# A selective scan with nine turned states, re-laid orders, and a row-wise walk of the column directions

## What is computed

```python
x_trans = jnp.transpose(xc, (0, 1, 3, 2)).reshape(Bn, Din, L)
x_hwwh = jnp.stack([x_flat, x_trans], axis=1)
xs = jnp.concatenate([x_hwwh, jnp.flip(x_hwwh, axis=-1)], axis=1)     # K = 4 directions
x_dbl = jnp.einsum('bkdl,kcd->bkcl', xs, x_proj_weight)
dts, Bs, Cs = jnp.split(x_dbl, [R, R + N], axis=2)                    # N = 16 states
delta = softplus(einsum(dts, dt_projs_weight) + dt_projs_bias)        # Din = 384
def step(h, inp):
    dA = jnp.exp(d_l[..., None] * A)
    dBu = d_l[..., None] * B_l[:, :, None, :] * u_l[..., None]
    h = dA * h + dBu
    y = jnp.sum(h * C_l[:, :, None, :], axis=-1)
```

## Time and profile before

| | |
|---|---|
| median of 3 runs | 28435.44 us (28420.39 to 28436.43) |
| the profiled execution | 28430.92 us |
| its span on the core | 28429.4 us |
| busy in the span: PE, DVE, ACT, POOL | 89%, 84%, 73%, 78% |
| mean granted TensorE clock | 0.944 of full speed |

### The profile page before, as it was taken

The page is one execution under the profiler, slowest core; times in us unless marked ns, Lnnn a source line. Parts: engine busy times, 40 slices in busy tenths (PEclk is TensorE's granted clock), DMA queues, the critical chain, the costliest instruction groups (busy, mean ns, idle before and its releaser), DMA issues. The chain is left out here.

```text
span 28429.4 us, 291694 instructions
## 1 busy us (share of the span) xinstructions
PE 25357.2 (89%) x80480; PEld 11869.3 (42%) x80480; DVE 23856.0 (84%) x23376; ACT 20735.5 (73%) x38376; POOL 22128.3 (78%) x9798
## 2 busy tenths in 40 slices
PE   8899888998889988899888998889988899888998
PEld 3444334443344433444334443344433444334443
DVE  6799867998679986799867998679986799867998
ACT  4788647886478864788647886478864788647886
POOL 3799737997379973799737997379973799737997
PEclk8999989999899998999989999899998999989999
DMA  0111101111011110111101111011110111101111
GB/s 8 51 63 64 45 8 51 63 64 45 8 51 63 63 46 8 51 63 63 46 8 51 63 63 46 8 51 63 64 45 8 51 63 64 45 8 51 63 64 45
DMA packets 833671, 1309.75 MB, mean 46 GB/s; under 512 B 224897, under 2 KB 242177, under 8 KB 828929
## 3 DMA queue, kind: packets, MB, share of 16 engines
q1 hardware_dynamic: 832000, 1290.45, 14.6%
HBM read 1223.00 MB, written 67.11 MB: 45 GB/s over the span
## 5 line engine op out<-in xcount | busy, mean ns | idle before, releaser
L1592 PE MATMUL ps<-arena,ident 128*128 128x512 f32 x24576 | 11670.0, 601 | 50.9 <-DVE arena L1419 50.8
L1407 DVE TENSOR_TENSOR_SCAN arena<-ps,arena 128x512 f32<-128x512 f32 x6144 | 7492.6, 1261 | 329.5 <-issue 208.0
L1407 DVE TENSOR_TENSOR_SCAN arena<-arena,ps 128x512 f32<-128x512 f32 x6144 | 7413.5, 1257 | 121.7 <-ACT arena L1786 101.9
L1960 POOL TENSOR_TENSOR arena<-arena 128x1536 f32<-128x1536 f32 x2048 | 7067.8, 3457 | 146.2 <-DVE arena L1407 144.6
L1592 PEld LDWEIGHTS ps<-arena,ident 128*128 128x128 f32 x24576 | 4349.8, 192 | 4544.5 <-issue 4240.7
L1970 POOL TENSOR_TENSOR arena<-arena 128x1536 f32<-128x1536 f32 x1728 | 5971.4, 3463 | 52.8 <-ACT arena L1806 52.8
L1797 ACT ACTIVATE scaled<-arena,cols 128x384 f32<-128x384 f32 x8192 | 4711.4, 605 | 1032.5 <-PE ps L1560 1025.5
L1786 ACT ACTIVATE ps<-arena 128x512 f32<-128x512 f32 x6144 | 4123.6, 684 | 602.2 <-DVE arena L1407 592.6
L1786 ACT ACTIVATE arena<-arena 128x512 f32<-128x512 f32 x6144 | 4251.2, 716 | 100.1 <-PE ps L1592 99.0
L1560 PE MATMUL ps<-ident,scaled 128*128 128x128 f32 x24576 | 3612.6, 277 | 590.3 <-DVE arena L1407 420.1
L1560 PEld LDWEIGHTS ps<-ident,scaled 128*128 128x128 f32 x24576 | 2854.6, 141 | 3050.1 <-DVE arena L1407 1583.7
(11 more groups left out here) (187 smaller groups left out, 32595.1 us busy)
## 6 DMA issues: line engine op xcount, KB each, us to landing
arena<-rows SPq DMA_DIRECT2D x3776, 256.0 KB, 3.2
spare<-rows SPq DMA_DIRECT2D x576, 256.0 KB, 3.4
arena<-x SPq DMA_DIRECT2D x16, 1536.0 KB, 13.0
x<-arena SPq DMA_DIRECT2D x16, 1536.0 KB, 10.7
arena<-x SPq DMA_DIRECT2D x64, 384.0 KB, 8.7
out<-arena SPq DMA_DIRECT2D x64, 384.0 KB, 3.0
rows<-xd SPq DMA_DIRECT2D x256, 64.0 KB, 2.7
arena<-L_conv_fc_w SPq DMA_DIRECT2D x16, 576.0 KB, 5.2
```

The lines of the kernel that those rows point to most:

```text
L1407: nc.vector.tensor_tensor_scan(flip(states(b, n, t)), flip(decays), flip(adds), carry[:, k, N2 * n + t:N2 * n + t + 1], ALU.mult, ALU.add) ...
L1592: nc.tensor.matmul(m.ps[:, t, :], m.ident[:, :], states(b, n, t), start=False, stop=(n == SUMS[t][-1])).then_inc(at[Y_MM[t]], 1)
L1960: nc.gpsimd.tensor_tensor(three(dbu[:, no % DB, :]), du[:, b % 2, :, :], each, ALU.mult).then_inc(at["db_ready"], 1)
```

## The change

Three things change, all in the scan.

1. TURNED grows from eight states to nine, (1, 3, 5, 6, 8, 9, 11, 13, 14). States 6 and 8 are new in it, 7 leaves. PLAIN is then (0, 2, 4, 7, 10, 12, 15). POOL_C keeps its nine states.
2. The per-block lists of all five engines and the orders SUMS are laid anew.
3. In the column directions the operands are walked by image rows. On the image side a pattern now reads eight neighbouring floats and jumps to the next row; its counterpart (PSUM for `rows_of`, `take_old` and `give_y`, SBUF for delta and du) is then stepped by 64 floats. Before, the image side was stepped by 64 floats and the counterpart was contiguous. The values are the same.

```diff
-TURNED = (1, 3, 5, 7, 9, 11, 13, 14)
+TURNED = (1, 3, 5, 6, 8, 9, 11, 13, 14)
-SUMS = ((1, 0, 2, 3, 4, 5, 6, 7, 8, 9, 10, 12, 11, 13, 14, 15),
...
+SUMS = ((0, 1, 2, 4, 3, 6, 5, 7, 8, 9, 10, 11, 12, 13, 14, 15),
...
         wide = T // H
-        return v.rearrange("p t (h w) -> p t w h", w=W)[:, t, i * wide:(i + 1) * wide, :]
+        return v.rearrange("p t (h w) -> p t h w", w=W)[:, t, :, i * wide:(i + 1) * wide]
 
     def shaped(b, v):
-        return v if b // NT % 2 == 0 else v.rearrange("p (w h) -> p w h", h=H)
+
+        return v if b // NT % 2 == 0 else v.rearrange("p (w h) -> p h w", h=H)
...
                 scan(b, 5, 2)
-                correct(ahead, 0)
-                times_c(b, 4)
                 scan(b, 6, 0)
                 scan(b, 6, 1)
                 scan(b, 6, 2)
+                correct(ahead, 0)
+                times_c(b, 4)
...
                 times_c(b, 0)
                 times_c(b, 1)
-                times_b(b, 6)
+                low_of(ahead)
+                times_b(b, 7)
                 times_c(b, 3)
-                times_b(b, 8)
+                times_b(b, 10)
                 softplus(ahead, 0, 0)
```

More of the change, by code:

```diff
@@ L1473, in _ @@
                 scan(b, 6, 2)
+                correct(ahead, 0)
+                times_c(b, 4)
                 scan(b, 7, 0)
                 scan(b, 7, 1)
[L1476 removed]
                 scan(b, 7, 2)
+                times_c(b, 6)
                 scan(b, 8, 0)
                 scan(b, 8, 1)
[L1480 removed]
                 scan(b, 8, 2)
+                correct(ahead, 1)
                 scan(b, 9, 0)
@@ L1596, in _ @@
                 past, ahead = b - 1, b + 1
+                add_up(past, 12, 2)
+                add_up(past, 12, 1)
+                rows_of(ahead, 0)
                 add_up(past, 11, 0)
-                rows_of(ahead, 0)
+                rows_of(ahead, 1)
                 turn_back(b, 1, 0)
-                rows_of(ahead, 1)
-                spread_c(past, 15)
+                rows_of(ahead, 2)
                 turn_back(b, 1, 1)
                 turn_back(b, 1, 2)
-                rows_of(ahead, 2)
+                add_up(past, 13, 2)
@@ L1613, in _ @@
                 turn_back(b, 3, 1)
                 turn_back(b, 3, 2)
+                take_old(b, 0)
+                spread_c(b, 2)
                 add_up(past, 14, 2)
                 add_up(past, 15, 1)
+                add_up(b, 0, 0)
                 delta_of(ahead, 0)
-                take_old(b, 0)
-                spread_c(b, 2)
-                add_up(past, 15, 2)
+                turn_back(b, 5, 0)
                 take_old(b, 1)
-                add_up(b, 1, 0)
-                turn_back(b, 5, 0)
@@ L1624, in _ @@
-                spread_c(b, 4)
                 turn_back(b, 5, 1)
                 turn_back(b, 5, 2)
-                add_up(b, 1, 1)
                 add_up(b, 0, 1)
                 take_old(b, 2)
+                add_up(b, 0, 2)
+                turn_back(b, 6, 0)
+                turn_back(b, 6, 1)
+                turn_back(b, 6, 2)
+                add_up(b, 2, 2)
+                spread_c(b, 4)
+                add_up(b, 1, 0)
+                add_up(b, 1, 1)
+                add_up(b, 1, 2)
@@ L1642, in _ @@
[L1642 to L1655, removed]
+                turn_back(b, 8, 0)
@@ new lines, in _ @@
+                add_up(b, 4, 0)
+                turn_back(b, 8, 1)
+                turn_back(b, 8, 2)
+                add_up(b, 3, 0)
+                spread_c(b, 8)
+                add_up(b, 4, 1)
+                add_up(b, 3, 1)
+                turn_back(b, 9, 0)
+                turn_back(b, 9, 1)
+                add_up(b, 6, 2)
+                turn_back(b, 9, 2)
+                add_up(b, 5, 1)
+                delta_of(ahead, 2)
+                add_up(b, 6, 0)
+                add_up(b, 5, 0)
@@ L1822, in _ @@
                 past, ahead = b - 1, b + 1
+                scale(b, 1, 2)
+                save(past, 14)
+                scale(b, 1, 3)
+                decay(b, 0, 0)
+                decay(b, 0, 1)
+                decay(b, 0, 2)
                 decay(b, 1, 0)
+                save(past, 15)
                 decay(b, 1, 1)
                 decay(b, 1, 2)
-                save(past, 15)
                 scale(b, 3, 0)
-                decay(b, 2, 0)
-                save(b, 0)
-                decay(b, 2, 1)
                 scale(b, 3, 1)
                 scale(b, 3, 2)
+                scale(b, 3, 3)
                 keep_rows(ahead)
+                save(b, 0)
+                decay(b, 2, 0)
+                decay(b, 2, 1)
                 decay(b, 2, 2)
-                scale(b, 3, 3)
+                decay(b, 3, 0)
+                high(ahead)
+                decay(b, 3, 1)
+                decay(b, 3, 2)
                 save(b, 1)
-                decay(b, 3, 0)
-                decay(b, 3, 1)
-                high(ahead)
-                decay(b, 3, 2)
+                give_y(past, 0)
                 save(b, 2)
-                give_y(past, 0)
                 scale(b, 5, 0)
@@ L2017, in _ @@
                 softplus(ahead, 2, 0)
-                times_b(b, 15)
                 softplus(ahead, 2, 1)
@@ L2021, in _ @@
                 times_c(b, 11)
+                times_b(b, 15)
                 times_c(b, 12)
```

194 lines of the change are left out of this document (91 added, 103 removed).

## The result

The changed kernel takes 27993.33 us (median of 4; 27982.7 to 28001.02) against 28427.92 beside it on the same chip: ratio 0.9847, 95% interval 0.9834 to 0.986.

A forecast was written before the change was run, and what follows sets the result against it. VectorE was taken to bound the scan, with GpSimd as full. Of 1.44 us idle per block 0.30 would remain; 1.14 x 256 = 291 us off 28430.92 gives 28140 us, range 28040 to 28380.

The forecast's parts named there:

- What bounds the kernel, and that the gaps go: In the scan: VectorE almost full; its gaps of 0.82 to 0.88 us before states 5 and 6 would go.
- VectorE works 70.56 of them: Scan block of 72.00 us: VectorE busy 70.56, idle 1.44, so at most 368 us to gain over 256 blocks.
- the low end of the range: 28040 us: no VectorE idle time at all, with start and end of eight scans allowed for.
- the sum: Idle time 1.44 less 0.30 left, 1.14 us per block times 256: 291 us gained, giving 28140.
- I leave 0.3 us of waits per block: VectorE waits remaining in each scan block after the change: 0.3 us, bounds 0 and 0.65.
- The walk: Column directions: TensorE records fall from about 1.03 us towards 592 ns, freeing 5.2 us per block; ScalarE gets back 1.4.
- a clock below 1.00: Sign in scan stretches: a granted clock under 1.00 would make the forecast wrong on the slow side.
- stops being a bound: Ninth turned state: GpSimd loses one times_b, 3.45 us per block, falling from 70.70 to 67.3.
- The rival for that case: PSUM steps cost as SBUF steps do: records stay at 1.03 us, column blocks take 71.9; 28272 us, chance 0.16.
- The margins: Walk through one block: slack of 0.05 to 0.4 us on ScalarE, 0.2 on TensorE; feasible but thin.

The follow-up runs named there:

- the wait of 1.05 for `scale` filled: Kernel before with new walk and delta_of(ahead, 1) behind three sums, plus the spread of C for state 6 issued five times: 28098.01 us, ratio 0.9886.
- the late delta: Kernel before with delta_of(ahead, 1) moved behind the three sums of states 0 and 1: 28620.43 us alone, 28314.19 us together with the new walk.
- The doubled product: Changed kernel with GpSimd's product times_b(b, 12) made twice, output the same: 28618.74 us, ratio 1.0066 against the kernel before.
- A wait of 1.36 us put into ScalarE's list: Changed kernel with rest_of moved from VectorE to GpSimd, just ahead of low_of: 28216.12 us, ratio 0.9926 against the kernel before.
- the smallest edit: Kernel before with only delta_of(ahead, 1) moved behind the three sums of states 0 and 1 on TensorE: 28620.43 us, ratio 1.0064.

## Why the prediction was wrong, and where it was right

**What bounds the kernel, and that the gaps go: right.** VectorE is the bound, its gaps in the earlier trace rows vanished, and the kernel that moved `rest_of` early shows it from the other side: 0.58 us taken off VectorE's list is 0.59 off each block.

**"VectorE works 70.56 of them": the step that failed first.** I took busy time per block as the floor, and 1.44 x 256 = 368 us as the most that could be had; the low end of the range, 28040, rests on it. The measured gain is 434.6, and the kernel reached 70.35. Instructions on VectorE overlap by some 0.09 us: the product in the earlier trace rows lasts 1.74, and its follower starts 1.65 to 1.67 later when nothing is waited for (1130.98 and 1132.65 in the timeline after). Busy time counts that overlap once where instructions touch, but before a gap the product's last 0.09 stand alone and look like work. So each gap costs its length and 0.09 more: 0.82 + 0.09 is the 0.91 between 71.26 and 70.35, and 0.24 + 0.09 the 0.33 between 70.68 and 70.35. On the sum: (70.56 - 70.35) x 256 = 54 us.

**"I leave 0.3 us of waits per block": the second failed step.** There are none: 0.3 x 256 = 77 us. The 0.3 rested on the irregular part of the idle time of before, 0.34 per block of the direction k = 0, which I called irregular and did not trace. It has two sources. Two of the eight blocks (TensorE's waits at 1273.46 and 1416.98) hold the slow clock, and VectorE idles 1.69 or 1.70 in each instead of 0.82, which is 1.74/8 = 0.22 per block. The last one already has the column direction's gap of 0.88, 0.11 per block. The walk takes away the second, and the first did not come in the changed kernel. Over the first sample seven of thirty blocks had it, 0.97 us each; that is an estimate of 7/30 x 0.97 x 256 = 58 us of the whole gain, for a cause that the sum has no term for. The prediction names a clock below 1.00 only as a sign of being wrong, and gives no reason why the changed kernel should be free of it; that it is was luck.

That a wait of TensorE brings the slow clock is shown for one place: with the wait of 1.05 for `scale` filled, none of the thirty blocks had it. The length of a wait alone doesn't decide it. The changed kernel no longer has the 0.95 before `delta_of(ahead, 1)`, but it has one of 1.02 us in each block elsewhere, for VectorE, and stays at 1.00 behind it:

```profile
1243.85 0.66 PE L1561 MATMUL ps<-ident,scaled 128*128 128x128 f32 x4 [1.02 <-DVE arena L1408]
```

```profile
1240.00:1250.00 10.00, 8.58 (x30) 4.07 (x29) 10.00 (x9) 7.16 (x15) 10.00 (x4) 1.00 0.19 59
1250.00:1260.00 10.00, 9.91 (x33) 4.59 (x31) 10.00 (x9) 9.03 (x19) 9.63 (x4) 1.00 0.44 138
```

What distinguishes the blocks in which the same wait brings it (seven of the kernel before, 11 of thirty with the new walk, 18 with the late delta) from the others stays open, and so does whether the changed kernel is free of it because the wait of 0.95 has gone; no run took that apart. 54 + 77 of the missing 144 us are these two steps. 13 are left: between two `correct(ahead, 0)` the blocks of before last 72.08 and not 72.00, which would be 20, so the sum closes to some 10 us.

**The ninth turned state "stops being a bound" for GpSimd: right.** I gave its block as 67.3; it is 2093.51/31 = 67.5. What that was worth I had not priced, and it is shown in part. In the old order, with the wait filled, the old load cost 0.1 to 0.5 us in some column blocks. In a block of 70.35 a column direction's old load of 568.03/8 = 71.0 could not have fitted; (71.0 - 70.35) x 128 = 83 us is an estimate of the least that it would have cost. The doubled product cost 625, where 90 to 160 were expected, but it stands elsewhere in the list than the product that was taken away. The new order was not run with eight turned states.

**The walk: right, and the Trainium skill's rule did not hold here.** TensorE's records in column blocks fell from 1.03 to 0.59 and `give_y` from 1066 to 576 ns. The Trainium skill says in "SBUF — State Buffer" (Door 1, the note on cachelines) that SBUF is read at full speed when a line of 16 bytes gets at least two hits; this is borne out for runs of eight floats, at 592 and 593 ns a record. That any non-contiguous PSUM pattern slows matmuls significantly, as the Trainium skill has it in the same note and in "PSUM — Partial Sum Buffer" (Specifications), is not borne out: 593 ns with a step of 256 bytes, 592 without, for float32 operands. Faster formats were not tried. The walk alone was worth 114 us, its absence in the changed kernel 171. The rival for that case gave 28272; measured 28164, since column blocks took 71.6, not 71.9, and row blocks 70.35, not 70.86.

**The margins: right that they are thin, wrong that waits had to be left for them.** A wait of 1.36 us put into ScalarE's list cost 1.29 of them; within the list as it stands every one of them held.

**What was not foreseen at all:** that removing the gap by the smallest edit would make the kernel slower. The sum had only looked at who waits for the gap, not at what becomes of TensorE's clock and of the waits behind it when its list changes.

## What to carry to other kernels

An engine's floor is the distance between starts in a stretch without waits, times the count; busy time next to gaps is too high. When a gap comes irregularly, list the blocks by length and look at the granted clock in short windows before calling it noise: here the seven blocks of the kernel before that were a microsecond too long were the seven with the slow clock in them. Then try filling TensorE's wait just ahead: in one order that gave 216 us. Not every wait of that length brings the slow clock. When one engine is at 100%, the next gain is an instruction moved off it, and its place in the new list decides: 3.4 us earlier turned a loss of 223 us against the changed kernel into a gain of 135.

## What the runs showed of the hardware that was not expected

- A TensorE wait of 1.05 us was followed by the lower clock level, 1.2 GHz, in 18 of thirty blocks (0.95 and 0.88 in two windows of 10 us of one of them), and such a block took 1.7 us more; with the wait at 0.18 us the clock stayed at 2.4 GHz in every block but the first sample's last. A wait of 0.95 us was followed by it in seven of thirty blocks of the kernel before and in 11 of thirty with the new walk, at 0.97 us a block. In the changed kernel a wait of 1.02 us per block goes without it.
- PSUM steps of 256 bytes cost nothing here in float32 matmul writes (593 ns against 592) and in ScalarE's copy (576 ns against 585); SBUF steps of 256 bytes do (1040 against 593 ns for `take_old`, 1054 to 1066 for ScalarE's `give_y`, by kernel).
- GpSimd's product of 128 x 512 takes 1534 ns with two stepping operands and 1536 with one, 1273 with none.
